# Attention by pairs of heads: probabilities transposed by 64 rows for both heads in one block with the scores; residual adds on GpSimd, hidden tiles in PSUM

## What is computed

```
L0: x += g * (gelu(mod(ln(x)) @ w1) @ w2)        hidden 256   phase 0
    x += g * (gelu(mod(ln(x)) @ w1) @ w2)        hidden 512   phase 1
L1: q, k, v = mod(ln(x)) @ W_qkv                 16 heads of 64
    x += g * (softmax(q @ k.T / 8) @ v) @ W_out               phase 2
    x += g * (gelu(mod(ln(x)) @ W1) @ W2)        hidden 1024  phase 3
L2: x += g * where(mask, fwd + bwd, 0)           hidden 512   phase 4
    x += g * (gelu(mod(ln(x)) @ w1) @ w2)        hidden 512   phase 5
L3: x += a1 * (softmax(Q @ K.T / 16) @ V)        one head     phase 6
    x += a2 * gelu(gelu(mod(ln(x)) @ W1) @ W2)   hidden 1024  phase 7
```

## Time and profile before

| | us |
|---|---|
| median of 3 runs | 1868.88 (1866.92 to 1870.78) |
| profiled execution | 1867.47 |
| its span, first to last instruction | 1865.3 |
| TensorE busy | 1740.8 |
| VectorE busy | 1353.7 |
| ScalarE busy | 1144.6 |
| GpSimd busy | 874.6 |

### The profile page before, as it was taken

The page is one execution under the profiler, slowest core; times in us unless marked ns, Lnnn a source line. Parts: engine busy times, 40 slices in busy tenths (PEclk is TensorE's granted clock), DMA queues, the critical chain, the costliest instruction groups (busy, mean ns, idle before and its releaser), DMA issues.

```text
span 1865.3 us, 36668 instructions
## 1 busy us (share of the span) xinstructions
PE 1740.8 (93%) x12739; PEld 1575.0 (84%) x12739; DVE 1353.7 (73%) x3357; ACT 1144.6 (61%) x2858; POOL 874.6 (47%) x949
## 2 busy tenths in 40 slices
PE   5888979999999999999999989999889979989998
PEld 3557869999999999999999879998778978879997
DVE  5878957777777777777777655557999879985663
ACT  3544646766666666666766565556556646666664
POOL 2545746666666666666666623333334523331111
PEclk7999989999999999999999999999999989999999
DMA  8222300000000000000000001111111112220111
GB/s 293 60 59 71 91 21 4 10 10 10 10 10 10 10 7 10 10 5 10 10 10 10 7 20 41 29 29 30 43 42 42 54 29 44 43 58 23 46 46 46
DMA packets 110970, 65.87 MB, mean 35 GB/s; under 512 B 81531, under 2 KB 92789, under 8 KB 110789
## 3 DMA queue, kind: packets, MB, share of 16 engines
q1 hardware_dynamic: 110788, 63.54, 12.6%
HBM read 59.06 MB, written 4.46 MB: 34 GB/s over the span
## 4 chain that ended last, share of the span: by engine, by line
PE 77%; DVE 10%; issue 6%; ACT 4%; POOL 1%; DMA 1%; DVEq 0%; POOLq 0%; SPq 0%; ACTq 0%
PE bank L255 21%; PE bank L257 20%; PE bank L256 20%; PE bank L1037 7%; PE bank L986 6%; PE bank L379 2%; DVE xn L342 2%; DVE hl L578 1%; PE bank L439 1%; ACT nf L392 1%; DVE nTlo L400 1%; ACT nThi L392 1%; DVE aTlo L400 1%; ACT hh L572 1%; DVE upd L609 1%
## 5 line engine op out<-in xcount | busy, mean ns | idle before, releaser
L1024 POOL TENSOR_SCALAR prob<-prob,rinv 128x256 f32<-128x256 f32 x512 | 468.8, 927 | 311.3 <-DVE rinv L1018 310.1
L572 ACT ACTIVATE hf<-bank,vecs 128x512 f32<-128x512 f32 x240 | 167.9, 700 | 306.0 <-PE bank L257 305.9
L578 DVE TENSOR_TENSOR hl<-hf,hh 128x512 fp32r<-128x512 f32 x240 | 196.3, 819 | 160.0 <-ACT hh L572 159.5
L999 DVE TENSOR_REDUCE nmax<-bank 128x2 f32<-128x512 f32 x256 | 175.7, 686 | 134.3 <-PE bank L986 134.3
L1009 ACT ACTIVATE prob<-bank,nmax 128x256 f32<-128x256 f32 x544 | 253.7, 479 | 29.8 <-DVE nmax L1284 21.6
L1046 ACT ACTIVATE pthi<-bank 128x512 fp32r<-128x512 f32 x272 | 164.7, 605 | 172.3 <-PE bank L1037 169.3
L334 POOL TENSOR_TENSOR rstd<-vareps,mhalf 128x2 f32<-128x2 f32 x128 | 106.1, 829 | 341.4 <-DVE vareps L330 340.7
L256 PE MATMUL bank<-WBlo,hh 128*128 128x256 f32 x768 | 217.9, 284 | 0.0
L257 PE MATMUL bank<-WBhi,hh 128*128 128x256 f32 x768 | 217.9, 284 | 0.0
L255 PE MATMUL bank<-WBhi,hl 128*128 128x256 f32 x768 | 217.5, 283 | 0.0
L255 PE MATMUL bank<-aThi,WAlo 128*128 128x256 f32 x576 | 175.9, 305 | 20.8 <-DVE aTlo L400 11.4
(11 more groups left out here) (164 smaller groups left out, 5274.1 us busy)
## 6 DMA issues: line engine op xcount, KB each, us to landing
gates<-gate_scratch SPq DMA_DIRECT2D x96, 256.0 KB, 3.7
agate<-gate_scratch SPq DMA_DIRECT2D x32, 256.0 KB, 3.2
stage<-in_L_cond_W SPq DMA_DIRECT2D x64, 64.0 KB, 2.2
out<-x SPq DMA_DIRECT2D x16, 256.0 KB, 2.2
adaw<-in_L_cond_Wc SPq DMA_DIRECT2D x1, 3072.0 KB, 17.8
stage<-in_L_cond_W_qkv SPq DMA_DIRECT2D x8, 384.0 KB, 3.4
x<-in_x SPq DMA_DIRECT2D x1, 2560.0 KB, 16.3
stage<-in_L_cond_ff_w SPq DMA_DIRECT2D x32, 64.0 KB, 2.1
```

What stands on the lines that cost most here:

```text
L572: last = act.activation(dst[:, :], U_BANKS[c % 2][:, :], ACTF[p], bias=vecs[:, at:at + 1])
L578: dve.tensor_tensor(hl[r][:, :], hf[r][:, :], hh[r][:, :].bitcast(F32), ALU.subtract).then_inc(h_lo, 1)
L999: dve.tensor_reduce(nmax[i][:, :], src.rearrange("p (q k) -> p q k", q=TPB), AX_X, ALU.max, negate=True).then_inc(nmax_ready, 1)
L1024: last = pool.tensor_scalar(dst[:, q, :], dst[:, q, :], rinv[i][:, q:q + 1], None, ALU.mult)
```

## The change

**Attention.** The unit of work is now a pair of heads. Probabilities have four buffers in place of two. In the period of pair n TensorE runs one block: half of the transposes of pair n (`pair_transpose`, turn 0), the scores of pair n + 2, the other half (turn 1). A transpose takes 64 rows of one head, with 64 moving columns; the other head's stands beside it with the other 64 rows and the other bank. Then come projections for a later pair, LN transposes, the output projection of pair n - 1, and the values of both heads. Scores were up to two heads ahead of the transposes and are two pairs ahead.

**LN.** The affine copy in float32 is written over its PSUM bank; `nf` is gone. In phase 2 it is made by DVE (`rows_vector`). The epsilon is added on GpSimd, and rsqrt is one instruction for two sequences where two are ready. In phase 6 normalisation is on GpSimd.

**FF.** The float32 hidden chunk is written over U, which has four banks; `hf` is gone, and Y has one set. The residual adds of all phases, the attention ones too, are on GpSimd. In phase 4 DVE keeps the predicated copy alone, straight into x. The gate row of the attention is double. Memsets that only spaced DVE's instructions are gone.

```diff
-        meanvar = [sb(f"meanvar{j}", [P, TPB, 2]) for j in range(GB)]
-        vareps = [sb(f"vareps{j}", [P, TPB]) for j in range(GB)]
-        rstd = [sb(f"rstd{j}", [P, TPB]) for j in range(GB)]
-        mhalf = sb("mhalf", [P, TPB])
+        meanvar = sb("meanvar", [P, GB, TPB, 2])
+        vareps = sb("vareps", [P, GB, TPB])
+        rstd = sb("rstd", [P, GB, TPB])
+        mhalf = sb("mhalf", [P, GB, TPB])
...
+        def ln_rsqrt(pool, p, b, j, n=1):
             u = p * BATCH + b
-            dve.wait_ge(ln_rstd, u + 1)
+            pool.wait_ge(ln_mv, u + n)
+            pool.tensor_scalar(vareps[:, j:j + n, :], meanvar[:, j:j + n, :, 1], EPS[p], None, ALU.add).then_inc(ln_ve, n)
+            pool.wait_ge(ln_ve, u + n)
+            pool.tensor_tensor(rstd[:, j:j + n, :], vareps[:, j:j + n, :], mhalf[:, j:j + n, :], ALU.pow).then_inc(ln_rstd, n)
...
-                for dst in (nf[j][:, c * SEQ:(c + 1) * SEQ], hi[c]):
+                for dst in (hi[c], T[:, c * SEQ:(c + 1) * SEQ]):
...
-        U_BANKS, Y_BANKS = bank[0:2], [bank[2:4], bank[4:6]]
+        U_BANKS, Y_BANKS = bank[0:HRING], bank[4:6]
...
-            if not early(n, 2):
-                pe.wait_ge(h_act, n - 1)
+            if not early(n, HRING):
+                pe.wait_ge(h_lo, n + 1 - HRING)
...
-            for dst in (hf[r], hh[r]):
-                last = act.activation(dst[:, :], U_BANKS[c % 2][:, :], ACTF[p], bias=vecs[:, at:at + 1])
+            for dst in (hh[r], U_BANKS[r]):
+                last = act.activation(dst[:, :], U_BANKS[r][:, :], ACTF[p], bias=vecs[:, at:at + 1])
...
-            if c == 0 and not early(GROUP_BASE[p] + g, 2):
-                pe.wait_ge(y_taken, GB * (GROUP_BASE[p] + g - 1))
             for r in range(GB * TPB):
-                last = split3(pe, Y_BANKS[i][r // TPB][:, (r % TPB) * D:(r % TPB + 1) * D],
+                if c == 0 and r % TPB == 0 and not early(GROUP_BASE[p] + g, 1):
+                    pe.wait_ge(y_taken, GB * (GROUP_BASE[p] + g - 1) + r // TPB + 1)
+                last = split3(pe, Y_BANKS[r // TPB][:, (r % TPB) * D:(r % TPB + 1) * D],
...
+        def ff_add(pool, p, g):
+            for j in range(GB):
                 n = GB * (GROUP_BASE[p] + g) + j
                 b = GB * g + j
                 if p == L3_FF:
-                    dve.wait_ge(gated2, n - GB * GROUP_BASE[L3_FF] + 1)
-                    dve.tensor_tensor(xs(b), xs(b), act2[:, j, :], ALU.add).then_inc(x_new, 1)
+                    pool.wait_ge(gated2, n - GB * GROUP_BASE[L3_FF] + 1)
+                    pool.tensor_tensor(xs(b), xs(b), act2[:, j, :], ALU.add).then_inc(x_new, 1)
                     continue
-                dve.wait_ge(y_taken, n + 1)
-                dve.wait_ge(xb_ready, n + 1)
+                pool.wait_ge(y_taken, n + 1)
+                pool.wait_ge(xb_ready, n + 1)
                 if p == L2_SSM:
-                    dve.memset(spacer[:, 2 + j:3 + j], 0.0)
-                    dve.tensor_copy(act2[:, j, :], xs(b))
-                    dve.tensor_copy(mcur[:, j, :], maski[:, bass.ds(b * TPB, TPB)])
-                    dve.tensor_tensor(upd[:, j, :], upd[:, j, :], xb[:, j, :], ALU.add).then_inc(x_tmp, 1)
-                    dve.wait_ge(x_tmp, 2 * b + 1)
-                    dve.memset(spacer[:, 4 + j:5 + j], 0.0)
-                    for k in range(TPB):
-                        last = dve.copy_predicated(act2[:, j, k * D:(k + 1) * D],
-                                                   mcur[:, j, k:k + 1].to_broadcast([P, D]),
-                                                   upd[:, j, k * D:(k + 1) * D])
-                    last.then_inc(x_tmp, 1)
-                    dve.wait_ge(x_tmp, 2 * b + 2)
-                    dve.memset(spacer[:, 6 + j:7 + j], 0.0)
-                    dve.tensor_copy(xs(b), act2[:, j, :]).then_inc(x_new, 1)
+                    pool.tensor_tensor(act2[:, j, :], upd[:, j, :], xb[:, j, :], ALU.add).then_inc(x_tmp, 1)
                 else:
-                    dve.tensor_tensor(xs(b), upd[:, j, :], xb[:, j, :], ALU.add).then_inc(x_new, 1)
+                    pool.tensor_tensor(xs(b), upd[:, j, :], xb[:, j, :], ALU.add).then_inc(x_new, 1)
+        def ff_where(dve, p, g, batches=range(GB)):
+            for j in batches:
+                b = GB * g + j
+                dve.wait_ge(x_tmp, b + 1)
+                for k in range(TPB):
+                    last = dve.copy_predicated(x[:, b * ROWW + k * D:b * ROWW + (k + 1) * D],
+                                               maski[:, b * TPB + k:b * TPB + k + 1].to_broadcast([P, D]),
+                                               act2[:, j, k * D:(k + 1) * D])
+                last.then_inc(x_new, 1)
...
-        PROJ_AT = {1: ("qk", 3), 2: ("v", 1, 0), 3: ("qk", 4), 4: ("v", 1, 1), 5: ("qk", 5), 7: ("qk", 6), 9: ("qk", 7),
-                   11: ("qk", 0), 12: ("v", 0, 0), 13: ("qk", 1), 14: ("v", 0, 1), 15: ("qk", 2)}
+        PROJ_AT = [[("qk", 4)], [("qk", 5), ("v", 1, 0)], [("qk", 6), ("v", 1, 1)], [("qk", 7)],
+                   [("qk", 0)], [("qk", 1), ("v", 0, 0)], [("qk", 2), ("v", 0, 1)], [("qk", 3)]]
+        NEXT = 4
...
+        def pair_transpose(pe, n, turn):
+            if turn == 0:
+                pe.wait_ge(prob_ready, 2 * n + 2)
+                if n:
+                    pe.wait_ge(pt_lo, 2 * n)
+            else:
+                pe.wait_ge(pt_half, 2 * n + 2)
             for c in range(TPB):
                 for q in range(TPB):
-                    last = pe.transpose(PTB[i][:, c * SEQ + q * P:c * SEQ + (q + 1) * P],
-                                        src[:, q, c * P:(c + 1) * P], ident[:, :])
+                    both = []
+                    for h in range(2):
+                        r = (h + turn) % 2
+                        rows = slice(r * HALF, (r + 1) * HALF)
+                        at = c * SEQ + q * P + r * HALF
+                        both.append(pe.transpose(PTB[h][:, at:at + HALF],
+                                                 prob[(2 * n + h) % 4][rows, q, c * P:(c + 1) * P], ident[rows, rows]))
+            for ins in both:
+                ins.then_inc(pt_mm if turn else pt_half, 1)
...
+        def rows_vector(dve, b):
+            u = A * BATCH + b
+            T = t_bank(A, b, 0)
+            dve.wait_ge(ln_nf, u + 1)
+            for c in range(DC):
+                cols = T[:, c * SEQ:(c + 1) * SEQ]
+                last = dve.tensor_scalar(cols, cols, mod[:, A, 0, c, b:b + 1], mod[:, A, 1, c, b:b + 1], ALU.mult, ALU.add)
+            last.then_inc(ln_full, 1)
+            dve.wait_ge(ln_full, b)
+            dve.tensor_tensor(aT[1][:, :, :], T[:, :].rearrange("p (c r) -> p c r", c=DC),
+                              aT[0][:, :, :].bitcast(F32), ALU.subtract).then_inc(ln_lo, 1)
...
+        def mh_tensor(pe, b, j):
+            n = PAIRS * b + j
+            pair_transpose(pe, n, 0)
+            if n + 2 < PERIODS:
+                pair_scores(pe, n + 2)
+            pair_transpose(pe, n, 1)
+            for it in items(b, j):
+                proj_tensor(pe, *it)
+            if j == NEXT - 1 and b + 1 < BATCH:
+                pe.wait_ge(proj_lo, item(b, ("v", 1, 1)) + 1)
+                ln_transpose(pe, A, b + 1, 0)
+            if b == BATCH - 1 and j == PAIRS - 1:
+                pe.wait_ge(proj_lo, NPROJ * BATCH)
+                for k in range(GB):
+                    head_unit("tensor", pe, A + 1, k)
+            if n:
+                out_project(pe, n - 1, (n - 1) % PAIRS, (n - 1) // PAIRS)
+            for h in range(2):
+                head_values(pe, b, 2 * j + h)
+            if n == PERIODS - 1:
+                out_project(pe, n, j, b)
...
+        def mh_vector(dve, b, j):
+            n = PAIRS * b + j
+            if n + 1 < PERIODS:
+                for h in range(2):
+                    prob_inverse(dve, 2 * n + 2 + h)
+            if j == 1 and b:
+                res_vector(dve, A, b - 1, YB, out_mm, PAIRS * b, b - 1)
+            if n:
+                o_rest(dve, n - 1, (n - 1) % 2)
+            for h in range(2):
+                if n + 2 < PERIODS:
+                    score_max(dve, 2 * n + 4 + h)
+                pt_rest(dve, 2 * n + h)
+            if j == NEXT - 1 and b + 1 < BATCH:
+                rows_vector(dve, b + 1)
+            for it in items(b, j):
+                proj_vector(dve, *it)
+            if b + 1 < BATCH:
+                if j == 1:
+                    ln_stats(dve, A, b + 1, 0)
+                if j == 2:
                     ln_norm(dve, A, b + 1, 0)
...
+        def mh_gpsimd(pool, b, j):
+            n = PAIRS * b + j
+            if n + 1 < PERIODS:
+                prob_weigh(pool, 2 * n + 2)
+            if j == 2 and b + 1 < BATCH:
+                ln_rsqrt(pool, A, b + 1, 0)
+            if b == BATCH - 1 and j == PAIRS - 3:
+                head_norms("gpsimd", pool, A + 1)
+            if n + 1 < PERIODS:
+                prob_weigh(pool, 2 * n + 3)
+            if j == 1 and b:
```

(10 more changed lines are left out.)

474 lines of the change are left out of this document (215 added, 259 removed).

## The result

The changed kernel takes **1786.49 us** (median of 4 runs, 1785.71 to 1787.64), the kernel before, run beside it, 1867.9 (1864.08 to 1870.78): ratio 0.9566, 95% interval 0.9547 to 0.9585. The forecast was 1779 us with a range from 1752 to 1829. The profiled execution took 1785.71 us with a span of 1783.9.

What follows compares the result with a forecast made beforehand. The prediction took TensorE (93% busy) to bound the kernel, though not masked phase 4. Its terms, -48 + 11 - 7 - 4 - 27 - 3 - 8 - 10 + 7 = -89 us, gave 1779 us, range 1752 to 1829.

Steps and rivals of the forecast that it cites:

- Transposes, -48: Attention by pairs: eight 64-row steps at 0.062 us replace eight transposes at 0.109, saving 0.376 us a pair, -48 us.
- rival of one-by-one issue: Small transposes issue singly, 0.124 us a step, kernel 1842; part of the rival that 64-row transposes save nothing, 18%.
- No more changes of mode: Attention block: still two changes between 128-row and 64-row work a pair, so no gain and no loss.
- Weighing late, +11: Attention by pairs: GpSimd's weighing fits by 0.6 us in short pairs, yet 0.7 us an image allowed for delays, +11.
- The stall for aTlo, -7: Attention by pairs: TensorE's 0.46 us stall once an image goes, since a value block now lies between, -7 us.
- Start of the attention, -4: Before the first weighed probabilities: extra scores and a projection fill TensorE's idle time; half the gain taken, -4 us.
- Phase 4, -27: Masked feed-forward: add moves to GpSimd, groups fall to TensorE's 12.2 us, phase from 124.9 us by -27.
- Y single, "hidden by 0.9 us": Feed-forward groups: TensorE's wait for the take is hidden by 0.9 us; without cover, 1 us in each of 48 groups.
- phase 5's first group: Feed-forward phase 5: first group takes 15.2 us while the last masked add is made; shortening it gives -3 us.
- Phases 0 and 1, the rest: First two phases: VectorE loses adds and small operations; half of phase 1's idle time and 2 us of phase 0, -8.
- Phase 6, -10: Single-head attention: normalisation and residual add move to GpSimd, removing a 0.74 us TensorE stall a turn, -10 over 14 turns.
- Ends, +7: GpSimd residual adds lengthen feed-forward and attention ends and the last store; joint rsqrt delays some four starts, 0.8 each: +7.

Runs made afterwards that it cites:

- e1: Changed kernel with each head's probabilities transposed in whole 128x128 steps, order and buffers kept: 1832.1 us, ratio 0.9818 to the kernel before.
- e2: Changed kernel with both heads' small transposes in each step on the same row half: 1832.4 us, ratio 0.9821 to the kernel before.
- e4: Changed kernel with all 16 small transposes of a pair together and the scores moved behind the projections: 2014.4 us, ratio 1.0794 to the kernel before.
- e5: As e4, but VectorE makes both subtractions for pT ahead of the two score maxima: 1929.6 us, ratio 1.0345 to the kernel before.
- e3: Changed kernel with GpSimd weighing only 2 of each 256 columns of the probabilities: 1781.5 us, ratio 0.9554 to the kernel before.
- f2: Changed kernel with two sets of Y banks again and two banks instead of four for the hidden part: 1779.3 us, ratio 0.9526.
- f1: Changed kernel with VectorE's cast of the second weight slice moved behind the take of Y in the second group: 1776.2 us, ratio 0.9505.
- f5: Changed kernel with the rsqrt of two images made one by one, T bank of phase 0 left single: 1781.3 us, ratio 0.9546.
- h1: Changed kernel with f1, single rsqrts, phase 0's first LN units in Y's banks, last residual adds of phases 1, 2, 5, 6, 7 on VectorE: 1762.7 us.
- g1: Changed kernel with phase 6's normalisation and residual add on VectorE again: 1794.3 us, ratio 0.9620 to the kernel before.

## Why the prediction was right, and where not

The sum was forecast at -89 and the span fell by 81.4 us; the direction and the place of the gain were right. Its terms:

- **Transposes, -48: right.** The step is 0.060 us where 0.062 was taken, and e1 takes 45.6 us back. By the Trainium skill, "TensorE: Matmul & The Clock Gate", section "LDWEIGHTS (loading the stationary operand)", a load takes its columns over 1.2 GHz, which I estimate at 107 ns for 128 columns; the steps of 0.060 us in the block and of 0.062 in e2, at a granted clock of 1.00, contradict it. The rival of one-by-one issue is e2: it would have given 1832, not 1842, since the first score matmul moves up.
- **No more changes of mode: right.** One in and one out a pair as before. e4 and e5 price another pair of them at 0.38 us; with the hand-over between the turns (0.30) it is 0.68 us a pair, 87 us in all, more than the transposes gain.
- **Weighing late, +11: wrong, it is 0.** The forecast let small delays of VectorE add up in spite of a slack that it had worked out itself; no wait for prob stands between the first pair and the last but one, and e3 leaves the image at 47.4. The forecast's own image of 47.5 us was that without this term.
- **The stall for aTlo, -7: right.** The image fell by 3.46 us, from 50.89 to 47.43; e1's 2.69 and the 0.46 are 3.15 of it, the other 0.3 is not told apart.
- **Start of the attention, -4: too much.** The stretch to the last take fell by 56.7 us; 16 images at 3.46 are 55.4, so the start and the end together gave about 1. The first transposes of probabilities stand 17.7 us behind the last take of phase 1, 18.6 before: 0.9 where the forecast took 4. The end was in no term: there the joint rsqrt ahead of a weighing costs TensorE a wait of 4.3 us (1017.94 us). No run takes it away.
- **Phase 4, -27: mechanism right, 4 too much.** Its groups take 12.5 us and not 12.2, and f2, with Y double, has 12.2: the take costs 0.3 us in each group, and once 1.7.
- **Y single, "hidden by 0.9 us": the step that failed.** It holds where it was read, in phase 3 (163.5 us before and after) and phase 7. In phases 0, 1, 4 and 5 VectorE has other things ahead of the take, a weight slice that waits for its transfer most of all, and TensorE waits 16.4 us. f2 puts the price at 12 us over phases 1, 4 and 5. The forecast had named waits of the first output for the take as a sign of being wrong. In phase 1 it is 5.2 of the 11.2 us that phases 0 and 1 are worse than forecast (-8 against +3.2), in phase 5 3.6 of 4.8 (-3 against +1.8). The cover was worked out from the earlier trace rows, which show phase 3 alone; the kernel before has VectorE idle for 3.47 us ahead of a take of phase 1, and the forecast has no term for that. The same slice explains phase 5's first group: the forecast put its 15.2 us down to the last masked add, but it takes 15.2 us in the changed kernel too, and 12.5 in f1.
- **Phases 0 and 1, the rest.** The joint rsqrt was priced at 0.8 us a start; f5 shows 3.3 for the start of phase 0, where two groups in a row hang on it. The T bank's longer hold was named and not priced: 1.4. The last group of phase 1 takes 12.7 us where it took 9.3, and in f2, f5 and h1 it is still 12.5 to 12.6. These rows stand in it, of VectorE and of TensorE:

```profile
244.92 2.62 DVE L339 TENSOR_SCALAR xn<-x,meanvar,rstd 128x256 f32<-128x256 f32 x2 [0.73 <-POOL rstd L331]
```

```profile
247.60 0.82 PE L380 MATMUL bank<-ident,xn 128*128 128x128 f32 x4 [2.59 <-DVE xn L339]
```

  GpSimd makes both residual adds (241.34 to 243.89 us) ahead of the rsqrt, and xn takes 2.62 us for two instructions, beside GpSimd's xb, where 0.73 stood before. That these two make the group longer is not tested by a run.
- **Phase 6, -10: 13.7.** 10.3 from the move (g1).
- **Ends, +7: 7.2.** The terms were not measured one by one; h1, with the last adds on VectorE, gives back 4.1 us, and the forecast had 4.3 for these adds.

The misses are of both signs, which is why the sum is closer than its terms, and that is luck: against the forecast the attention by pairs came out 8.7 us better and phase 6 3.7, phases 0, 1, 4 and 5 together 19.9 worse.

## What to carry to other kernels

Transposes or matmuls that fill only half of the rows pay off when two of different row halves alternate; one by one they cost as much as whole ones (e1, e2). When a double buffer is given up, the cover has to be read in every phase: what else stands ahead of the freeing instruction on its engine, above all waits for transfers; in one phase the price was 0, in another 5.5 us at once. Two small operations joined into one wait for the later of their inputs: the joint rsqrt cost 3.3 us at the start of phase 0. An operation that is moved on one engine drags the in-order queue of the others with it: e4 lost some 1.1 us a pair only because VectorE had the maxima ahead of a subtraction that TensorE needed first.

## What the runs showed of the hardware

- The two row halves of TensorE need not go in step: with all transposes of a turn on one half, a score matmul started at 601.68 us, ahead of a transpose at 601.74 that stands before it in the program (e2).
- The first step after a change to 64-row work, or after a wait (707.12 us in e5), takes 0.11 us, the later ones 0.060 to 0.062, for transposes that load 128 stationary columns.
- The small transposes of the second turn, which write the banks of the first from the other row half, start 0.31 us after the start of the last of the first turn when nothing stands between (e5). The kernel orders them by a semaphore, so this is the hand-over, not a property of the array.
- After the pause of 5.49 us in phase 1, TensorE's 256-column matmuls start 0.21 us apart instead of 0.12, the lower of its two clocks (1.2 GHz) (165.33 and 165.55 in the rows of the waits above); the granted clock from 165.00 to 165.70 us is 0.50, over phase 1 it is 0.94, over phase 4 1.00. So this wait cost more than its length.
- ScalarE's activation written back into its own PSUM bank costs no more than one into SBUF, as the page's groups show (count, busy time, mean ns of one):

```profile
L573 ACT ACTIVATE hh<-bank,vecs 128x512 fp32r<-128x512 f32 x240 | 167.6, 698 | 283.7 <-PE bank L254 283.4
...
L573 ACT ACTIVATE bank<-bank,vecs 128x512 f32<-128x512 f32 x240 | 159.5, 664 | 0.0
```
